# Masks of causal attention as matmuls on TensorE, paired heads in short steps, row maxima three units ahead

## What is computed

```python
mod = (silu(c) @ wmod).reshape(B, 6, 1, -1)         # shifts, scales and gates
h = layernorm(x) * (1 + ca) + sa
q, k, v = heads(h @ W_qkv.T + b_qkv)
scores = einsum('bnqd,bnkd->bnqk', q, k) * 16 ** -0.5
scores = where(triu(ones, k=1), -inf, scores)       # causal
x = x + ga * (softmax(scores) @ v @ W_out.T + b_out)
h = layernorm(x) * (1 + cb) + sb
x = x + gb * (routed_experts(h) + shared_expert(h)) # 4 of 16 experts for each token
```

## Time and profile before

| | us |
|---|---|
| three runs | 710.51, 720.26, 755.53 |
| median | 720.26 |
| the profiled execution | 709.61 |
| its span, first to last instruction | 706.9 |
| PE busy in it | 629.8 (89%) |
| DVE / ACT / POOL busy | 460.1 / 373.3 / 324.5 |
| TensorE clock, mean | 0.877 of full |

### The profile page before, as it was taken

One profiled execution on the slowest core, in us unless ns is written; L12 is line 12 of the kernel. 1 busy time (PEld: TensorE's weight loads), 2 busy tenths in 40 slices (PEclk: granted clock), 3 DMA queues, 4 the chain that ended last, 5 costly groups with the idle time before them and its releaser, 6 DMA issues. The chain is left out here.

```text
span 706.9 us, 13625 instructions
## 1 busy us (share of the span) xinstructions
PE 629.8 (89%) x4088; PEld 432.5 (61%) x4088; DVE 460.1 (65%) x1144; ACT 373.3 (53%) x910; POOL 324.5 (46%) x565
## 2 busy tenths in 40 slices
PE   2989699879999798988898997999789999999997
PEld 2776343434444344444444345787679999999985
DVE  4676866754577445746466617788856677667748
ACT  4254065644566344544364655365335677776663
POOL 5124051542635525582362758677414444444440
PEclk9999658995699659989669578999979999999999
DMA  8469855750617255164020322447595444444489
GB/s 273 153 214 288 320 127 164 188 181 2 155 65 185 100 92 191 37 156 164 31 106 32 140 80 84 144 168 239 210 366 183 137 138 128 134 135 138 130 317 344
DMA packets 58293, 113.85 MB, mean 161 GB/s; under 512 B 11726, under 2 KB 32654, under 8 KB 57072
## 3 DMA queue, kind: packets, MB, share of 16 engines
q1 hardware_dynamic: 51296, 93.97, 43.5%
q0 software_dynamic: 6864, 19.01, 7.0%
q10 hardware_dynamic: 64, 0.02, 0.0%
HBM read 60.57 MB, written 49.94 MB: 156 GB/s over the span
## 5 line engine op out<-in xcount | busy, mean ns | idle before, releaser
L1435 ACT ACTIVATE Pr<-bank 128x512 f32<-128x512 f32 (+3 forms) x384 | 163.7, 494 | 158.0 <-PE bank L2245 153.7
L1578 DVE TENSOR_REDUCE mxA<-bank 128x4 f32<-128x512 f32 (+2 forms) x96 | 99.3, 1046 | 76.4 <-PE bank L2126 75.6
L2245 PE MATMUL bank<-Qs,Ks 50*128 50x512 f32 (+3 forms) x384 | 126.0, 492 | 22.2 <-ACT Pr L1435 18.8
L1300 POOL DMA_INDIRECT expert_rows<-Y,YIX x79 | 75.8, 959 | 104.8 <-DVE ytmp L1989 73.3
L2245 PEld LDWEIGHTS bank<-Qs,Ks 50*128 50x128 f32 x384 | 60.5, 223 | 101.2 <-ACT Pr L1435 68.3
L2229 PE MATMUL bank<-Pr,Vst 128*32 128x512 f32 (+3 forms) x768 | 102.8, 616 | 8.5 <-POOL Pr L1284 8.5
L2126 PE MATMUL bank<-Ks,Qs 48*128 48x512 f32 (+3 forms) x384 | 104.6, 470 | 3.0 <-DVE mxA L1578 1.0
L1282 POOL TENSOR_TENSOR tick<-ident 128x1 f32<-128x1 f32 x128 | 26.1, 204 | 159.9 <-ACT Pr L1435 159.0
L1578 DVE TENSOR_REDUCE mxB<-bank 128x2 f32<-128x1024 f32 x64 | 78.2, 1223 | 29.5 <-PE bank L2126 28.5
L1234 POOL DMA_INDIRECT chosen_rows<-Hx,pos x64 | 70.8, 1106 | 22.3 <-issue 17.5
L2496 PE MATMUL bank<-W,xh 128*128 x316 | 78.7, 331 | 0.5 <-issue 0.5
(11 more groups left out here) (255 smaller groups left out, 1331.7 us busy)
## 6 DMA issues: line engine op xcount, KB each, us to landing
G<-chosen_rows SPq DMA_DIRECT2D x79, 132.0 KB
...
```

The costliest lines, as they stand in the source:

```text
L1300: nc.gpsimd.indirect_dma_start(out=zd, out_offset=bass.IndirectOffsetOnAxis(ap=YIX[:, b:b + 1], axis=0), in_=Y[b % YRING], in_offset=None) ...
L1435: nc.scalar.activation(Pr[(2 * s + j // 2) % 4][:, j % 2, 0:w], ebank[p % RING][:, 0:w], ACT.Exp, scale=SCALE).then_inc(exp_done, EXP)
L1578: nc.vector.tensor_reduce(dst, src, AX.X, ALU.max).then_inc(read_of(piece), 1)
L2245: nc.tensor.matmul(ebank[p % RING][:, 0:CH - q0], Ks[slot][rows, a, kt * P:(kt + 1) * P], Qs[slot][rows, qc, a, q0:CH], start=True, stop=T ...
```

## The change

- POOL's masks and `tick` are gone. Ahead of the score matmuls of a diagonal step PE writes a mask into each bank (weights `mask`, the identity streamed against it, 128 rows, bf16), and the score matmuls add to it, so the exponential gives zero there.
- The mask of a diagonal unit is one matmul over 128 rows for each of the two banks, in place of two over 64 rows; `swapped` and its two DMAs are gone.
- Scores are issued for two heads at once (`g`), with both waits ahead of both. In steps of 256 and 128 columns the four heads share two banks, two heads in each, so there are two exponentials in place of four. An iteration has 40 exponentials (`NI`) in place of 48.
- Units run three ahead (`AHEAD`): iteration n computes units 3 to 19 of n + 1 and 0 to 2 of n + 2. Both halves of the maxima of n + 1 are turned and written in iteration n.
- The stream ahead of iteration 0 (`FIRST_STREAM`) starts behind the last read of the projection's banks, runs three units further, and has three 128-row matmuls of 512 columns behind each unit, into a bank that nobody reads.

The diff, cut to its core:

```diff
+AHEAD = 3
+FIRST_IDLE = 3
+assert len(ROWS) == NS and AHEAD < FIRST_HALF
+def first_query(s):
+    qc, kt = STEPS[s]
+    return max(0, kt - TPC * qc) * P
...
+ITEMS, ITEMS_TO = [], []
+for _s in range(NS):
+    _groups = [(0, PAIRS)] if PAIRS * (CH - first_query(_s)) <= CH else [(a, 1) for a in range(PAIRS)]
+    ITEMS += [(_s, l, a, n) for a, n in _groups for l in range(SIDES)]
+    ITEMS_TO.append(len(ITEMS))
+NI = len(ITEMS)
...
-    unit_cost = [n * SIDES * (w + 100) for _, _, _, w, _, n in UNIT_LIST]
-    head_cost = [CH - max(0, kt - TPC * qc) * P + EXTRA for qc, kt in STEPS for _ in range(HG)]
+    unit_cost = [150 + n * SIDES * w for _, _, _, w, _, n in UNIT_LIST]
+    item_cost = [170 + n * (CH - first_query(s)) for s, _, _, n in ITEMS]
...
+def unit_of(n, i):
+    return n + 1 + (i + AHEAD) // UNITS, (i + AHEAD) % UNITS
 M_ORDER = (0, 2, 1, 3)
 QK_RING = 3
 PER = 1
 OVER = PER * (4 * KH + 4)
-START_PARTS = max(OVER, FIRST_HALF)
+FIRST_STREAM = [("unit", 0, OVER), ("parts", 0, 0), ("unit", 0, OVER + 1), ("max", 0, 0)]
+FIRST_STREAM += [("unit", 0, u) for u in range(OVER + 2, UNITS)] + [("parts", 0, 1), ("unit", 1, 0), ("max", 0, 1)]
+FIRST_STREAM += [("unit", 1, u) for u in range(1, AHEAD)]
+assert OVER >= FIRST_HALF
 LN_STEPS = 2 * TPC + 2
...
+                if first:
+                    was_read(sp, ("max", 0, 1))
+                    aug(sp, 0, 1)
                 for k in EARLY_LOADS.get(n, ()):
                     load_words(k)
                 if n + SLOTS - 1 < NIT:
-                    sp.wait_ge(e_ps, n * HEADS + 1)
+                    sp.wait_ge(e_ps, n * NI + 1)
                     sp.wait_ge(pv_done, n * NS + 1)
                     stage(n + (SLOTS - 1), (slot + SLOTS - 1) % SLOTS)
                     stage_values(n + (SLOTS - 1), (slot + SLOTS - 1) % SLOTS)
                 for k in EARLY_RAW.get(n, ()):
                     load_raw(k)
                 if not last:
-                    was_read(sp, ("max", n + 1, 0))
-                    aug(sp, (slot + 1) % SLOTS, 0)
+                    for half in range(2):
+                        was_read(sp, ("max", n + 1, half))
+                        aug(sp, (slot + 1) % SLOTS, half)
                 if n == 0:
                     keep_pads()
                 for k in EARLY_STORES.get(n, ()):
...
-                            k = masked_before(s) + pair
-                            pool.wait_ge(exp_done, n * (EXP * HEADS) + EXP * (HG * s + 2 * pair + 2))
-                            nc.gpsimd.tensor_tensor(tick[:, k:k + 1], ident[:, 0:1], ident[:, 0:1], ALU.mult)
-                            v = Pr[(2 * s + pair) % 4][:, :, 0:P]
-                            nc.gpsimd.affine_select(out=v, in_=v, compare_op=ALU.is_ge, fill=0.0, base=0,
-                                                    pattern=[[0, 2], [1, P]], channel_multiplier=-1).then_inc(masked, 1)
                     for piece in LATE_POOL.get((n, s), ()):
                         work(piece)
                     for k in PRE_POOL.get((n, s), ()):
...
+                        if start and not (n == 0 and s < 2):
                             act.wait_ge(pv_done, n * NS + (s - 1))
-                        if j == 0 and n == 0 and s == 1:
+                        if start and n == 0 and s == 1:
                             act.wait_ge(parts_out[0], 16 * TILE_DMAS * B)
-                        nc.scalar.activation(Pr[(2 * s + j // 2) % 4][:, j % 2, 0:w], ebank[p % RING][:, 0:w],
-                                             ACT.Exp, scale=SCALE).then_inc(exp_done, EXP)
-                        if j == 1:
+                        nc.scalar.activation(PrA[:, PAIRS * (s % 2) + a:PAIRS * (s % 2) + a + pairs, l, 0:w],
+                                             ebank[k % RING][:, 0:pairs * w].rearrange("p (a w) -> p a w", a=pairs),
+                                             ACT.Exp, scale=SCALE).then_inc(exp_done, 1)
+                        if l == 1 and a == 0:
                             for piece in LATE_ACT.get((n, s), ()):
                                 work(piece)
...
+                    for piece in FIRST_STREAM:
+                        {"unit": row_maximum, "parts": max_parts, "max": max_copy}[piece[0]](*piece[1:])
                     return
-                max_parts(n, 1)
                 if last:
-                    max_copy(n, 1, at(-1))
                     for s in range(NS):
                         if s == 3:
                             normalise(n * 2 - 1)
...
-                    for part in range(2):
-                        for l in range(SIDES):
-                            rows, k = slice(SIDE * l, SIDE * (l + 1)), P if part == 0 else SIDE
-                            table = (plain, swapped)[part ^ l]
-                            to = bank[:, l, 0:pairs * w].rearrange("p (a w) -> p a w", a=pairs)[:, :, w - k:w]
-                            nc.tensor.matmul(to, table[rows, 0, :],
-                                             table[rows, 1:2, P - k:P].broadcast_to([SIDE, pairs, k]), start=part == 0, stop=False,
-                                             skip_group_check=True)
+                    for l in range(SIDES):
+                        to = bank[:, l, 0:pairs * w].rearrange("p (a w) -> p a w", a=pairs)[:, :, w - P:w]
+                        nc.tensor.matmul(to, identb, plain[:, 1:2, :].broadcast_to([P, pairs, P]), start=True, stop=False,
+                                         skip_group_check=True)
                 for a in range(first, first + pairs):
                     for l in range(SIDES):
                         rows = slice(SIDE * l, SIDE * l + NPR)
...
                                            start=(kt == 0), stop=(kt == TPC * (qc + 1) - 1), skip_group_check=True)
                 ins.then_inc(pv_done, 1)
-            def scores(n, slot, turn, p):
+            def scores(n, slot, turn, g):
+                s, _, first, pairs = ITEMS[SIDES * g]
+                (qc, kt), q0, diag = STEPS[s], first_query(s), on_diagonal(s)
+                w = CH - q0
+                bank = [ebank[(n * NI + SIDES * g + l) % RING] for l in range(SIDES)]
+                for l in range(SIDES):
+                    k = n * NI + SIDES * g + l
+                    if k >= RING:
+                        pe.wait_ge(exp_done, k - RING + 1)
+                    if diag:
+                        to = bank[l][:, 0:pairs * w].rearrange("p (a w) -> p a w", a=pairs)[:, :, 0:P]
+                        nc.tensor.matmul(to, mask, plain[:, 0:1, :].broadcast_to([P, pairs, P]), start=True, stop=False,
+                                         skip_group_check=True)
+                if kt == 0 and first == 0:
                     pe.wait_ge(aug_in[slot][qc], (turn + 1) * 16 * AUG_DMAS)
-                if n or p >= RING:
-                    pe.wait_ge(exp_done, n * (EXP * HEADS) + EXP * (p - RING + 1))
-                a, l = j // SIDES, j % SIDES
-                rows = slice(SIDE * l, SIDE * l + NAUG)
-                nc.tensor.matmul(ebank[p % RING][:, 0:CH - q0], Ks[slot][rows, a, kt * P:(kt + 1) * P],
-                                 Qs[slot][rows, qc, a, q0:CH], start=True, stop=True).then_inc(e_ps, 1)
+                for a in range(first, first + pairs):
+                    for l in range(SIDES):
+                        rows = slice(SIDE * l, SIDE * l + NAUG)
+                        ins = nc.tensor.matmul(bank[l][:, (a - first) * w:(a - first + 1) * w],
+                                               Ks[slot][rows, a, kt * P:(kt + 1) * P], Qs[slot][rows, qc, a, q0:CH],
+                                               start=not diag, stop=True, skip_group_check=True)
+                        if a == first + pairs - 1:
+                            ins.then_inc(e_ps, 1)
...
             def body(n, at, first, last):
                 if n == -1:
-                    for u in range(OVER, UNITS):
-                        score_unit(0, 0, u)
-                        if u == START_PARTS + 1:
-                            turn_max_waits(0, 0)
-                            turn_max(0, 0)
                     pe.wait_ge(v_read, 2 * NC)
                     qk_was_read(4 * NC - 1)
+                    for piece in FIRST_STREAM:
+                        if piece == ("unit", 1, 0):
+                            pe.wait_ge(staged[1], 16 * STAGE_DMAS)
+                        if piece[0] == "unit":
+                            score_unit(piece[1], piece[1], piece[2])
+                            for i in range(FIRST_IDLE):
+                                nc.tensor.matmul(pvb, Wqkh[:, 0, 0:P], hh[1][:, 0, :], start=True, stop=True)
+                        if piece[0] == "max":
+                            turn_max(piece[1], piece[2])
                     return
-                (slot, turn), (nxt, nxt_turn) = at(0), at(1)
+                (slot, turn), (nxt, _), (then, then_turn) = at(0), at(1), at(2)
                 pe.wait_ge(staged_v[slot], turn * 16 + 16)
```

(2 more changed lines are left out.)

170 lines of the change are left out of this document (63 added, 107 removed).

## The result

The changed kernel is slower: 735.6 us median (730.8 to 748.2) beside 720.4, a ratio of 1.037 with a 95% interval of 1.026 to 1.048. The forecast was 692. The executions of one kernel fall in a faster and a slower group, with a lower granted clock in the slower, and ratios compare the faster ones. The profiled execution took 742.3 us, 6.7 above the median, so a part of what that trace holds belongs to it alone; two more traces of the same kernel, from other executions (719.5 and 745.3 us), are used beside it.

What follows compares the result with a forecast made beforehand. PE was taken to bound the attention, by its work and the clock it runs at. From 709.6 us, 15 + 6 - 2 - 8.5 - 28.6 = -18.1 gave 691.5, forecast as 692; own range 677 to 708, with rivals 670 to 722.

Steps and rivals of the forecast that it cites:

- PE work (+15): Attention: masks on PE, joint waits and new order take a full-clock period from 32.35 to 34.2 us; +15 in all.
- the joint wait: Scores: head 2 now waits with head 3 for head 0's exponential, 1.23 us to the release in step 4.
- DVE's maxima lie beside PE's work: Stream ahead of iteration 0: DVE's maxima, some 1.2 us a unit, were taken to lie beside it.
- Stream and fillers (+6): Ahead of iteration 0: later start, eleven units and fillers put scores near 92 instead of 86.00 us; +6.
- Three units fewer in iteration 6 (-2): Iteration 6: three units are gone, worth -2 us.
- POOL's stalls (-8.5): Attention: PE's four waits for POOL's masks go, -8.5 us together, the longest 2.9.
- The clock (-28.6): Full clock from the stream into iteration 4, as the two long stalls go and the stream is filled; -28.6 us.
- POOL and ACT: Behind the attention POOL sends rows without a pause; nothing more, at most 1 us; ACT's fewer exponentials: nothing.
- D: Rival: the new wait in steps 1, 4, 6 and 9 costs the clock; 760 us, deciding from 735; chance 0.10.
- C: Rival: the clock falls as often as now, for other causes than the stalls; 720 us; chance 0.15.

Runs made afterwards that it cites:

- Experiments 2 and 4: Score masks alone on the kernel before: 703.1 us, ratio 1.001; old 64-row unit masks in the changed kernel with products between groups and residual earlier: 688.7 us.
- experiment 1: Kernel before with POOL's splitting of expert words cut into five pieces between masks: 684.1 and 697.0 us, ratios 0.965 and 0.973.
- experiment 4: Changed kernel with DVE's residual pieces of chunks 0 and 1 one unit earlier in iterations 4 and 5: 706.3 us, ratio 1.005.
- experiment 5: Changed kernel with products between groups, residual earlier, old unit masks, and POOL waiting for each step's exponentials in iteration 7: 683.7 us, beside 689.3 without those waits.

## Why the prediction was wrong, step by step

- **PE work (+15).** The direction was right, the size short. Steps measured 3.53, 3.22, 1.77, 2.54, 2.52, 3.14, 3.28, 3.58, 4.14, 4.60, 2.13 and 1.26 us against 3.55, 3.30, 1.77, 2.50, 2.17, 2.81, 3.15, 2.81, 4.30, 4.50, 2.11 and 1.24. Single mask matmuls start 0.066 us apart and the changes of tiling cost what was taken; nine steps are within 0.16. Steps 4, 5 and 7 hold 1.45 of the 1.5 us that were missed. In steps 4 and 5 (0.68) the step that failed is the joint wait: it was counted within step 4, but not from its last group to the next step's first (0.17 of idle time) nor within step 5 (0.22). In step 7 (0.77) it is an overlap taken for granted, that DVE's maxima lie beside PE's work: the step's second unit waits 0.37 us for one and so starts 0.53 later. Seven iterations make +10 of all three. Experiments 2 and 4 then say what the 3.4 us a period are: 2.8 score masks, some 2.2 unit masks, and by difference 1.6 back from shared banks and the order.
- **Stream and fillers (+6).** 6.6, 8.3 and 10.6 in the three traces; the fillers' part returns in iteration 0.
- **Three units fewer in iteration 6 (-2).** Not to be seen under the clock and the gap there.
- **POOL's stalls (-8.5).** Right, they are gone; experiment 1 shows that the two long ones and the half clock behind them were the kernel's to win, at 20 to 24 us, without the change.
- **The clock (-28.6).** This step failed. Iterations 1 and 2 came out at 35.7 us with the clock held, but "full clock from there into iteration 4" took for granted that only a long stall lets it fall. In the new order it falls in step 5 of one or two of the first four iterations with no wait over 0.54 us ahead (9 to 13 us each; why there, stays open beyond what moving the products shows), and in iterations 4 and 5 behind the residual's waits of 1.4 to 1.7 us, which were not in the sum at all (6.1 us of waits, 12 us in all by the two iterations in experiment 4).
- **Not foreseen:** the row of 16 sends that POOL's freed time makes. It was costed at nothing ("POOL and ACT"), and goes with a gap of 12.3 us in the profiled execution; what the gap costs isn't shown (experiment 5). Nor was it foreseen that iteration 7 gets shorter without POOL's masks (33.6 to 38.0 us instead of 41.7 in the three traces).
- **The rivals.** D had the sign and nearly the place: waits of 0.53 us in steps 4 and 6 instead of 0.28, and by its own bound it decides from 735. Its mechanism is not shown, since waits as long stand in the order that keeps the clock, and that 735.6 lies just over its bound is luck: its 40 us of lost clock were 9 to 13 a fall, and work, DVE's residual and that execution's own losses made up the rest. C (falls without a stall of POOL's) gave 720, by the work sum that was 10 short.

The balance of the first trace against the kernel before, from the table at the start: +8.3 ahead of the loop, -1.0, -4.7, -3.6, +4.4, +2.0, +5.9, +17.2 and -3.7 in iterations 0 to 7, +8.8 behind them, 33.6 together. The forecast's terms for iterations 0 to 2 come to -16.5 (+5.7 of work, -2.9 of stall, -19.3 of clock) and -9.3 was measured; that the clock held in 1 and 2 is that execution's luck, as the third trace shows. Between the forecast's -18.1 and the 33.6 lie 52 us, of which, as an estimate, 10 are work, 2 the stream, 9 the fall in iteration 3, 12 the residual in 4 and 5, and 17 what the second trace hasn't got (8.8 behind the attention, 8.4 in iteration 6).
